# Attention steps on one core: the order of the products with the weights and of the next scores

## What is computed

```python
# x: (4, 2048, 256), bq, bk, bv: signs of three vectors
Q = sign(x * bq); K = sign(x * bk); V = x * bv
scores = einsum('btd,bsd->bts', Q, K) * 256 ** -0.5
attn = where(causal, sigmoid(scores * 4.0), 0.0)
x = layernorm(x + einsum('bts,bsd->btd', attn, V))
# experts: T = 8192 tokens, 32 experts, top 1, at most C = 320 tokens each
probs = softmax(x @ w_router); top1 = argmax(probs)
y = (silu(buf @ w_gate) * (buf @ w_up)) @ w_down      # buf: the tokens of each expert
x = layernorm(x + gate * y)
```

## Time and profile before

| | before |
|---|---|
| time, median of 3 runs | 571.13 us (569.78 to 571.21) |
| time of the profiled execution | 569.9 us |
| its span, first to last instruction | 568.1 us |
| granted TensorE clock, mean over the span | 0.987 |
| TensorE busy (matmul) | 534.0 us, 94% |
| VectorE busy | 409.5 us, 72% |
| ScalarE busy | 375.7 us, 66% |
| GpSimd busy | 387.4 us, 68% |

### The profile page before, as it was taken

One profiled execution on the slowest core, in us unless ns is written; L12 is line 12 of the kernel. 1 busy time (PEld: TensorE's weight loads), 2 busy tenths in 40 slices (PEclk: granted clock), 3 DMA queues, 4 the chain that ended last, 5 costly groups with the idle time before them and its releaser, 6 DMA issues.

```text
span 568.1 us, 12280 instructions
## 1 busy us (share of the span) xinstructions
PE 534.0 (94%) x4024; PEld 471.0 (83%) x4062; DVE 409.5 (72%) x1027; ACT 375.7 (66%) x743; POOL 387.4 (68%) x544
## 2 busy tenths in 40 slices
PE   6999999999999999999999889999999999999970
PEld 5889897898888888888897369989999999998960
DVE  4785867957878766788557347888888877888860
ACT  5886867959587787787773235666666666666641
POOL 4646778678777778677771713677777777777772
PEclk9999999999999999999999999999999999999995
DMA  8994323234322533315710153666666566666300
GB/s 240 354 348 174 93 82 85 89 117 124 103 54 76 163 94 104 66 38 130 250 54 6 35 155 114 198 204 206 199 192 190 178 208 203 211 209 203 122 33 34
DMA packets 80638, 81.49 MB, mean 143 GB/s; under 512 B 20362, under 2 KB 71802, under 8 KB 80576
## 3 DMA queue, kind: packets, MB, share of 16 engines
q1 hardware_dynamic: 73504, 66.27, 38.8%
q0 software_dynamic: 6912, 14.30, 7.0%
q10 hardware_dynamic: 160, 0.13, 0.1%
HBM read 44.29 MB, written 37.90 MB: 145 GB/s over the span
## 4 chain that ended last, share of the span: by engine, by line
PE 76%; issue 6%; DVE 6%; POOL 5%; DMA 2%; ACT 2%; another core or an unknown queue 1%; SPq 0%; DVEq 0%; POOLq 0%; ACTq 0%
PE ps L892 10%; PE ps L893 10%; PE ps L894 10%; PE ps L868 9%; PE ps L1071 7%; PE ps L1043 7%; PE ps L1051 6%; PE ps L1044 6%; POOL out_dram L598 3%; PE ps L911 2%; PE ps L1021 2%; PE ps L1066 2%; PE ps L1067 2%; PE ps L1068 2%; DVE hl_ring L1136 2%
## 5 line engine op out<-in xcount | busy, mean ns | idle before, releaser
L892 PE MATMUL ps<-v_hl,hl_ring 128*128 128x256 f32 x544 | 176.1, 324 | 0.6 <-DVE hl_ring L1136 0.3
L893 PE MATMUL ps<-v_hl,hl_ring 128*128 128x256 f32 x544 | 153.4, 282 | 0.0
L894 PE MATMUL ps<-v_hl,hl_ring 128*128 128x256 f32 x544 | 153.1, 281 | 0.0
L598 POOL DMA_INDIRECT out_dram<-alone,ids x80 | 106.1, 1327 | 46.1 <-ACT alone L808 16.9
L892 PEld LDWEIGHTS ps<-v_hl,hl_ring 128*128 128x128 f32 x544 | 103.3, 190 | 15.8 <-issue 1.1
L1136 DVE TENSOR_TENSOR hl_ring<-ps,hl_ring 128x512 fp32r<-128x512 f32 (+3 forms) x160 | 93.5, 601 | 20.8 <-ACT ps L675 15.3
L893 PEld LDWEIGHTS ps<-v_hl,hl_ring 128*128 128x128 f32 x544 | 103.5, 190 | 2.4
L894 PEld LDWEIGHTS ps<-v_hl,hl_ring 128*128 128x128 f32 x544 | 103.2, 190 | 0.0
L673 ACT ACTIVATE hl_ring<-ps 128x512 fp32r<-128x512 f32 (+3 forms) x160 | 85.8, 536 | 24.8 <-PE ps L868 10.8
L675 ACT ACTIVATE ps<-ps 128x512 f32<-128x512 f32 (+3 forms) x160 | 86.9, 543 | 0.0
L505 POOL DMA_INDIRECT expert_rows<-xrow,slot x64 | 64.4, 1006 | 29.6 <-issue 22.1
(11 more groups left out here) (154 smaller groups left out, 1095.8 us busy)
## 6 DMA issues: line engine op xcount, KB each, us to landing
expert_rows<-xs SPq DMA_DIRECT2D x40, 258.0 KB, 8.8
xs<-expert_rows SPq DMA_DIRECT2D x32, 258.0 KB, 2.9
xall<-in_L_attn_x_dram SPq DMA_DIRECT2D x16, 512.0 KB, 3.9
out_dram<-alone SPq DMA_DIRECT2D x16, 512.0 KB
xall<-in_L_ffn_w_gate_dram SPq DMA_DIRECT2D x32, 256.0 KB
xall<-in_L_ffn_w_up_dram SPq DMA_DIRECT2D x32, 256.0 KB
xall<-in_L_ffn_w_down_dram SPq DMA_DIRECT2D x32, 256.0 KB
xs<-expert_rows SPq DMA_DIRECT2D x30, 64.5 KB, 3.1
```

The costliest lines, as they stand in the source:

```text
L598: g_.indirect_dma_start(out=out_rows, out_offset=bass.IndirectOffsetOnAxis(ap=ids[:, e % U, t:t + 1], axis=0), in_=o_s[:, p, t, :], in_off ...
L892: mm(o, ah, v_hl[:, 0, j, :], start=(j == 0 and i % 2 == 0), stop=False, skip_group_check=True)
L893: mm(o, ah, v_hl[:, 1, j, :], start=False, stop=False, skip_group_check=True)
L894: last = mm(o, al, v_hl[:, 0, j, :], start=False, stop=(j == GT * g + i), skip_group_check=True)
```

## The change

`values` keeps the two products with the high weights of each tile and waits for `ah_ready` alone. The products with the low weights go to a new function `values_low`, which waits for `al_ready` and raises `pv_done`. In each step TensorE now issues `values`, then the scores of step k + 4, then `values_low`; in the first two steps of the first batch `values_low` follows `values` at once.

```diff
@@ values @@
                 pe.wait_ge(ah_ready, n + 1)
-                pe.wait_ge(al_ready, n + 1)
                 for i in range(lo // P, GT):
...
                     ah = hl_ring[:, 0, r, i * P:(i + 1) * P]
-                    al = hl_ring[:, 1, r, i * P:(i + 1) * P]
                     mm(o, ah, v_hl[:, 0, j, :], start=(j == 0 and i % 2 == 0), stop=False, skip_group_check=True)
                     mm(o, ah, v_hl[:, 1, j, :], start=False, stop=False, skip_group_check=True)
-                    last = mm(o, al, v_hl[:, 0, j, :], start=False, stop=(j == GT * g + i), skip_group_check=True)
+
+            def values_low(b, k):
+
+                g, j, lo = cols(k)
+                r = k % WRING
+                pe.wait_ge(al_ready, b * NS + k + 1)
+                for i in range(lo // P, GT):
+                    last = mm(ps[:, PV + i // 2, (i % 2) * D:(i % 2 + 1) * D], hl_ring[:, 1, r, i * P:(i + 1) * P],
+                              v_hl[:, 0, j, :], start=False, stop=(j == GT * g + i), skip_group_check=True)
                 last.then_inc(pv_done, 1)
@@ batch @@
                     if first and k < 2:
                         values(0, k)
+                        values_low(0, k)
...
                     else:
+                        values(b, k)
                         if k + SB < NS:
                             scores(b, k + SB)
                         elif not last:
                             scores(b + 1, k + SB - NS)
-                        values(b, k)
+                        values_low(b, k)
```

## The result

| | before | after |
|---|---|---|
| time, median of 5 runs | 570.24 us (569.78 to 571.21) | 575.46 us (575.10 to 577.89) |
| ratio to before, 95% interval | | 1.0094 (1.0072 to 1.0116) |
| span of the profiled execution | 568.1 us | 573.5 us |
| last product of the attention starts | 307.85 us | 312.81 us |
| from there to the end of the span | 260.3 us | 260.7 us |

So 4.96 of the 5.4 us of the span arise in the attention. The experiments are judged by two numbers: the ratio, and where their attention ends.

The account below looks back on a forecast made before the run. TensorE was taken to bound the attention. Losses of 1.4 + 0.7 + 0.6 us, less 0.25 and 0.1, gave +2.35 us, which against the median 571.13 made 573.4 us, 0.4% slower; range 570.3 to 575.6 us.

Parts of the forecast that it names:

- the residual's lost cover: First products of tiles 2 and 3 await the second residual; work covering that wait falls from 1.15 to 0.48 us.
- late scores: Rival, chance 0.07: scores of step k + 4 start up to 0.96 us later; taken as 0, otherwise 5.8 us, 579.3.
- Where a group begins, steps 24 and 25: Four batches: tile 2 starts at E + 1.00 (E: end of step before); loss 0.37 us each, 1.4 taken.
- Steps 4 and 5: Three batches: TensorE resumes at E + 0.99 (E: end of step before); loss 0.21 us each, 0.6 in all.
- The mask (L871): Mask with the scores in steps 4 and 5: 0.05 us added to each step.
- Steps 0 to 3: Batches 2 to 4: TensorE stops for the second residual in step 0; loss 0.22 or 0.23 us each, 0.7 in all.
- the gap: Step 0: VectorE's second residual starts late near GpSimd's DMA; taken to stay; gone in two batches, 1.6 us replaces 2.35.
- The first batch: First product starts at 11.95 us instead of 12.37; after step 4's loss, 0.25 us gained by step 5's end.
- Switching: One bf16 to fp32r change per step as before; new borders between high and low products cost 0; other bound 16 us.
- signs of a wrong forecast: Full step above 1.87 us; new waits at transposes or router; second residual starting under 0.2 us after the step's end.
- the waits of the earlier trace: Scores waiting for low weights before the change: 3.5 us at most, of which 2.3 was counted as taken back.
- 0.40 us of idle time ahead of step 25: Read as step 25's scores (L868) waiting before the change; the pair took 0.25 us beyond its work; this wait goes.

Follow-up runs that it names:

- e5: The changed kernel with the scores last in each step, behind the products with low weights: 571.88 us, 1.0035 of before.
- e3: The changed kernel with scores first again in each group's first step and in steps 7, 9, 13, 18, 29, 31, 35: 568.71 us, 0.9976 of before.
- e10: As e4, but high products also first in seven steps not following other TensorE work (10, 15, 16, 19, 22, 33, 36): 567.47 us, 0.9958 of before.
- e1: The changed kernel with scores first again in the eight steps behind router, counts or turned logits: 573.18 us, 1.0053 of before.
- e9: As e4, but high products also first in seven steps following other TensorE work (7, 9, 13, 18, 29, 31, 35): 569.62 us, 0.9999 of before.
- e7: As e4, but with the scores last in each group's last step (3, 11, 23, 39): 566.35 us, 0.9944 of before.
- e8: The kernel before, with GpSimd's indirect DMAs of steps 39 and 0 moved into the next batch: 578.69 us, 1.0138 of before.
- e6: The changed kernel with scores first, then high, then low products, except in the first batch's steps 0 and 1: 569.89 us, 0.9981 of before.
- e4: As e6, but with high products ahead of the scores in steps 1, 2, 5, 25 and 34: 568.24 us, 0.9952 of before.

## Why the prediction was right where a group begins, and half in its size

Forecast 573.4 us against 571.13, +2.35 us; measured +5.2. The direction was right, and so was the mechanism that it had, the residual's lost cover. A second one, at the borders behind other work, wasn't in it and makes half of the loss. That 575.46 us still lies under the range's upper end, 575.6, is luck: that end was set for late scores, which cost nothing, and by the prediction's own terms a fourth of them gives 2.35 + 5.8 / 4 = 3.8 us, 574.9. By its own steps:

- **Where a group begins, steps 24 and 25**: right. Forecast 1.4 us, measured 1.87, of which 4 x 0.11 is the border behind the router; 1.43 is left.
- **Steps 4 and 5**, batches 2 to 4: forecast 0.6, measured 1.07. The stop is as forecast (tile 2 at E + 1.00 in all three). The mask (L871) was mis-sized: I took 0.05 us. Before, step 4 takes 93.49 - 91.50 = 1.99 us, 0.12 more than a full step; two masks give the missing 0.14 us in each batch.
- **Steps 0 to 3**, batches 2 to 4: forecast 0.7, measured -0.01. In the second and third batch the second residual starts 0.30 and 0.41 us behind the step's end, where it was 0.63 and 0.81 before, which wins 0.7 us against the forecast. The section on the gap had named this as possible and then taken the gap to stay; in the fourth, where there was none, the loss is 0.24 as forecast (0.23).
- **The first batch**, steps 0 to 5: forecast -0.25, measured -0.10. The first product starts at 11.77 us, even ahead of the 11.95 forecast; but in the ten kernels with this order it starts anywhere from 11.63 (e5) to 12.27 us (e3), so the fit is no test of this term.
- **Late scores**, taken as 0: right. e5 and e10 delay them as much or more and lose nothing by it.
- **Switching, "I take 0"**: this is the step that failed. Inside a step it is 0, as the earlier trace rows had it: full steps stay at 1.87 us, and e10 costs nothing. But the claim that a step has one change of type as before looked only inside the step: the term taken as 0 measures 2.57 us. The change also moved the step's first instruction, from a bf16 score to an fp32r product, and what follows the router or the counts pays for it. By the lines of the table it is 2.13 us outside of step 25 and 0.44 in it. e1 takes 2.1 of it away; e9's seven steps put 1.9 back.

The sum closes: 1.43 + 1.07 - 0.01 - 0.10 + 2.57 = 4.96 us, the attention's loss in the trace. Of the things named as signs of a wrong forecast none appeared as written: the border costs no wait at the router, and no full step is longer. It lay at a place where I had looked for new waits only.

Two readings of the prediction were wrong without harm to the sum: the waits of the earlier trace rows, as said above, and 0.40 us of idle time ahead of step 25, of which the sum rightly used only 0.25.

That the border's price is the uncovered weight load rests on the rows (0.19 against 0.11 us, spacing 0.22 against 0.12), and on e9 and e10 for its place. The graded price fits it: the products ahead stand 0.025 us apart in the router (0.11 us lost), 0.055 at the end of the counts (0.06) and 0.11 in the transposes and turned logits (nothing), so more of a load can be covered from one to the next. But the loads differ by 0.08 us, and the price behind the router is 0.11. No run changed the load and nothing else, so the load as the cause is argued and not shown.

## What to carry to other kernels

A reordering inside a loop also changes what stands at the loop body's first place; check what runs ahead of it there, and, if the load is the cause as argued, let an instruction with a cheap weight load follow small products. Work that covered a wait was worth more here than the wait that it was moved for: before moving instructions off the front of a queue, list for each wait behind them how much of its time they fill. Here the best order was not one order for all steps, but one chosen for three kinds of steps: scores first where a group begins or other work ran before, last where a group ends, and in between only where low weights are late. And count the rows of a trace before you trust an idle time in it: a missing row reads as waiting.

## What the runs showed of the hardware

- A high product right behind other work of TensorE costs 0.10 to 0.11 us more than a bf16 score there behind the router, and 0.06 to 0.07 behind the counts (steps 13 and 31, and 9, 18, 29 and 35, of e9), and 0.02 or less behind transposes of 0.11 us each (steps 12, 14, 21 and 30 of after).
- The trace of before has 285 rows for 320 scores: the first of two is missing, mostly where it stands behind other work or a wait. In after, e9, e10 and e7 all 320 are there.
- The second residual (VectorE, one input in PSUM) starts late in some batches, with the end of a GpSimd indirect DMA close by. Second residual and the DMAs around it, third batch of after:

```profile
161.45 0.68 DVE L1151 TENSOR_TENSOR xs<-ps,xall 128x512 f32<-128x512 f32 x1
162.76 0.69 DVE L1151 TENSOR_TENSOR xs<-ps,xall 128x512 f32<-128x512 f32 x1 [0.63 <-issue]
161.77 0.98 POOL L505 DMA_INDIRECT expert_rows<-xrow,slot  x1 [0.30 <-issue]
```

  The DMA ends at 162.75, the residual starts at 162.76; before, the distances are 0.09 and 0.08 us. e8 shows that without these DMAs there is no gap. But in e6, e5 and e4 the residual also starts, unhindered, in the middle of such a DMA (e5, second batch: start 85.65, DMA 85.25 to 86.23), and in the third batch of e4 it starts 0.9 us after its step's end, at no DMA's end. The DMAs have to do with the gap; by what rule it comes is open, and an exclusive hold for the whole DMA is not it.
